# Norm, statistics and moves of rows 3 to 5 reordered at the boundary of a two-stage fp32 layer, and the last element of its first stage

## Chip, cores and metric

The kernel runs on one core of one Trainium2 chip. The metric is the device time of one launch in microseconds (us), the median of the runs shown. It is written in Bass: every engine has its own instruction list in a fixed order, and engines meet only at semaphores, so the order in the source is the order on each engine.

## What is computed

Sixteen batch rows of 128 x 1024 fp32 go through two layers:

```
x = x + tanh(g_xattn) * xattn(layernorm(x), ctx, ctx, Wq, Wk, Wv, Wo, bo, g)
x = x + tanh(g_ffn)   * ffn(layernorm(x), A, B, Wr)

xattn: q = softmax(Wq q) over 64 channels of a head, k = softmax(Wk k) over 1024 positions
       context = k v^T;  out = Wo (context q) + bo
       out / max(sqrt(sum_c out^2), 1e-12) * g * sqrt(128)
ffn:   scores = x Wr^T; the top 16 of 64 experts, softmax over them = gates
       out = sum_k gates_k * B_k (A_k x), rank 16 each; times 2
```

## The kernel before

**Precision.** Every fp32 matmul is done as three passes over operands split into a high part (`_hi`) and a remainder (`_lo`): `three_pass`, lines 61 to 63. ScalarE or a casting DMA makes the high part, VectorE or GpSimd subtracts to get the low part. A matmul group therefore waits for a `lo` step.

**Stage one** (`body` on each engine, b = 0 to 16) does the attention of row b (its head) and the end of row b-1 (its tail). The attention output u of a row goes to DRAM (`u_scratch`). `body(15)` is the last with a head, `body(16)` has only the tail of row 15 and, between its pieces, the first work of stage two: on TensorE context(15), `tr_y(0)`, `tr_q`, `fold(15)` (ends with m_mm), then `up(0, 0)`, the first matmuls of row 0 of stage two. `up(0, 0)` waits for y_lo, which VectorE's `lo_y(0)` sets.

**Stage two** (`ffn_body`, b = 1 to 15) runs on TensorE as `up(b, 0)`, `up(b, 1)`, `up(b, 2)` and `down(b - 1)`: 72 and 48 matmuls. Around it, for row b:

- The norm of u of row e = b+2: ScalarE squares u (`square_u`: line 748 into usq, line 749 scales u), VectorE sums it (`part_u`, line 1190), TensorE adds over partitions with one small matmul pair (`sum_u`, line 1520), VectorE takes the reciprocal root in 11 steps (`norm_step`, lines 969 to 977 and 67, each 128x32) and spreads it (`spread`, line 992), GpSimd multiplies u by it and adds x (`residual`, lines 522 and 525) and so makes the row x2.
- The statistics of x2 on VectorE (`stats2`, lines 1060, 1062 and `std2`), the normalising on ScalarE (`normalise`, line 761), a turn of 32x32 blocks on VectorE (`turn_y`, 1150), 16 block moves on ScalarE (`move_y`, 776), high part (793) and low part (`lo_moved_y`, 1154). `up(b, 0)` waits for this low part.
- The gates on VectorE (`route`, 11 steps, lines 1087 to 1119), the gated product (`gated`, 1134), and the same turn, moves, high (802) and low part (`lo_moved_h`, 1172) for h. `down(b)` waits for this low part.

**The first rows are special.** Rows 0 and 1 get their norm early, with reciprocal roots by GpSimd (`early_newton`). For them VectorE spreads the root (`spread`, into rb_first[0] and rb_first[1]), GpSimd multiplies (`spread_first(e)`, line 506, ends with u_done) and adds x (`add_first(e)`, line 516, ends with x2_done). The tile x_second lies at the same address as rb_first[1]. SyncE fills it with x of row 1 only after u_done has reached 2:

```
sp.wait_ge(u_done, 1)
load(u_first[:, :], u_dram, 1, second_loaded)
sp.wait_ge(u_done, 2)
load(x_second[:, :], x, 1, xr_loaded[1])
```

`add_first(1)` reads x_second and waits for xr_loaded[1]. Behind it on GpSimd come `halve(15, 3)` (line 444), whose result VectorE's `sum_q(15, 3)` (line 1007) waits for, and `normalise(15, 2)` and `(15, 3)`. `lo_y(0)` on VectorE (line 1145) stands behind `sum_q(15, 3)` and itself waits for x2_done of row 1.

At the start of stage two GpSimd makes the low parts of six strips of B (`lo_b`, line 481, 128x1024 each, one behind the other) and VectorE those of two (line 1051).

Of the kernel before, what the change touches and what calls it, by code (L numbers as in the profile page):

```python
# [6 lines left out]
def flamingo_layer(nc, x, ctx, ctxT, g_xattn, g_ffn, WqT, WkT, Wv, WoT, bo, g, AT, BT, u_dram, turn_dram, out):  # L7
# [26 lines left out]
    NEWTON = 3  # L34
# [53 lines left out]
    with outer:  # L88
# [308 lines left out]
        def _(pool):  # L397
# [129 lines left out]
            def body(b, head, tail, ahead, split=False):  # L527
# [11 lines left out]
                if head and not ahead:  # L539
                    spread_first(0)  # L540
                if tail:
                    pool.wait_ge(m_hi, b)
                    nc.gpsimd.tensor_tensor(mts[1][:, :, :], mt[:, :, :], mts[0][:, :, :].bitcast(f32),
                                            ALU.subtract).then_inc(m_lo, 1)
                if split:
# [3 lines left out]
                if head and not ahead:  # L549
                    add_first(0)  # L550
# [3 lines left out]
                if head and not ahead:  # L554
                    for t in range(3):
                        hi_a(t)
                if ahead:
# [5 lines left out]
                if head and not ahead:  # L563
                    spread_first(1)
# [11 lines left out]
                if head and not ahead:  # L576
                    add_first(1)
# [42 lines left out]
        def _(act):  # L620
# [121 lines left out]
            def square_u(e, half, uses):  # L742
# [4 lines left out]
                act.wait_ge(n_part, e)  # L747
                nc.scalar.activation(usq[:, :], u_in[half][:, :], ACT.Square).then_inc(u_sq, 1)
                nc.scalar.activation(u_in[half][:, :], u_in[half][:, :], ACT.Copy,
                                     scale=gcol[:, 0:1]).then_inc(u_scaled, 1)  # L750
# [154 lines left out]
            def ffn_body(i, j):  # L905
# [12 lines left out]
                if not isinstance(i, int) or b <= NB - 4:  # L918
# [12 lines left out]
        def _(dve):  # L931
# [260 lines left out]

            def norm_u(e):

                before = NRT * (e - EARLY)
                for k in range(NRT):
                    norm_step(k, e - EARLY + 2, psN.unsqueeze(1), 1, before)
                dve.wait_ge(x2_done, e)
                spread(0, rb, n_step, before + NRT)
# [13 lines left out]
            def body(b, head, tail, ahead, early=False):  # L1213
# [17 lines left out]
                if tail and head:  # L1231
# [36 lines left out]
                if last:  # L1268
                    dve.wait_ge(xn_lo, 2 * NB)
                    spread(1, rb_first[1], n_newton, 4 * NEWTON)  # L1270
# [39 lines left out]
                if last:  # L1310
                    std2(0, range(4, NCH + 1))
                if head:
# [419 lines left out]
```

## Time and profile before

| what | value |
|---|---|
| median of 3 runs | 930.25 us (928.26 to 930.46) |
| the profiled execution, own time | 932.08 us |
| its span in the trace | 930.4 us |
| PE (TensorE matmul) busy | 901.6 us, 97% |
| DVE (VectorE) busy | 739.7 us, 80% |
| ACT (ScalarE) busy | 684.3 us, 74% |
| POOL (GpSimd) busy | 520.0 us, 56% |
| mean granted TensorE clock | 0.993 |

PEld is TensorE's weight load, SP is SyncE with its DMA queue. In the 40 slices of the page, TensorE is at 9 tenths or more in nearly all, with one slice of 6 tenths at about 605 to 628 us where the granted clock is also below full. Times below are microseconds from the start of the span. A row of the trace that ends in "[3.67 <-DVE yT_lo L1154]" tells how long the engine stood idle before it and what released it. Stage one ends at about 533 us, body(16) runs from there to 557 us, and `ffn_body(1)` starts at 557.07 us.

### The profile page before, as it was taken

The numbers are of one execution on the slowest core, as the hardware profiler recorded it, in microseconds if no ns is written. First come the engines' busy times: TensorE is split into PE (matmuls) and PEld (weight loads), VectorE is DVE, ScalarE is ACT, GpSimd is POOL, SyncE is SP. The second block draws the span as 40 slices with busy tenths as digits, with TensorE's granted clock in tenths as the row PEclk, the third lists the DMA queues.
The fourth block names the chain that finished last, engine by engine and source line by source line (L and its number), as shares of the span: only waits on it lengthen the run. The fifth ranks groups of instructions, "written<-read, shape, count | busy, mean of one in ns | idle before, by whom it ended". The sixth has DMA issues, their size and how long they took to land.

```text
span 930.4 us, 15943 instructions
## 1 busy us (share of the span) xinstructions
PE 901.6 (97%) x4732; PEld 764.7 (82%) x4732; DVE 739.7 (80%) x1523; ACT 684.3 (74%) x1400; POOL 520.0 (56%) x342
## 2 busy tenths in 40 slices
PE   7899999999999999999999999969999999999998
PEld 5687888878787787888887798869999999999896
DVE  6888889988888898898887778777777777777642
ACT  4787787777778777876876758687888888888731
POOL 3686778789778878977789856221222222222200
PEclk9999999999999999999999999979999999999999
DMA  4323423452453444233322784111111211111001
GB/s 158 114 91 125 173 103 124 161 173 100 161 182 106 146 137 159 90 137 135 119 89 87 230 329 154 46 68 68 69 69 68 69 68 68 68 68 68 23 24 46
DMA packets 35319, 104.04 MB, mean 112 GB/s; under 512 B 4432, under 2 KB 11600, under 8 KB 35280
## 3 DMA queue, kind: packets, MB, share of 16 engines
q1 hardware_dynamic: 29520, 82.59, 25.2%
q0 software_dynamic: 5472, 20.45, 6.9%
q10 hardware_dynamic: 288, 0.52, 0.2%
q8 instruction: 19, 0.31, 0.1%
q14 instruction: 20, 0.16, 0.1%
HBM read 79.43 MB, written 24.12 MB: 111 GB/s over the span
## 4 chain that ended last, share of the span: by engine, by line
PE 63%; DVE 9%; POOL 8%; issue 8%; ACT 7%; DMA 2%; SPq 0%; POOLq 0%; ACTq 0%; DVEq 0%
PE ps L61 19%; PE ps L63 18%; PE ps L62 18%; PE ps L1455 3%; PE ps L1464 3%; POOL qe L451 2%; ACT h_raw L776 2%; ACT qe L683 2%; POOL ctx_lo L410 2%; PE ps L1445 1%; DMA turn_scratch<-ek 1%; POOL qhalf L444 1%; POOL aT_lo L464 1%; ACT qT_hi L691 1%; DVE qmax L1002 1%
## 5 line engine op out<-in xcount | busy, mean ns | idle before, releaser
L522 POOL TENSOR_TENSOR rb<-u_in,rb 128x1024 f32<-128x1024 f32 x14 | 33.7, 2409 | 224.7 <-DVE rb L992 224.7
L451 POOL TENSOR_TENSOR qe<-qe,qrec 128x1024 f32<-128x1024 f32 x64 | 121.3, 1906 | 16.3 <-DVE qrec L1010 16.3
L61 PE MATMUL ps<-aT_hi,yT_hi 128*128 128x448 f32 (+2 forms) x360 | 121.1, 337 | 3.7 <-DVE yT_lo L1154 3.7
L62 PE MATMUL ps<-aT_hi,yT_lo 128*128 128x448 f32 (+2 forms) x360 | 119.7, 332 | 0.0
L63 PE MATMUL ps<-aT_lo,yT_hi 128*128 128x448 f32 (+2 forms) x360 | 119.4, 332 | 0.0
L776 ACT ACTIVATE h_raw<-hg 32x256 f32<-32x256 f32 x248 | 103.0, 415 | 16.8 <-DVE hg L1159 14.0
L444 POOL TENSOR_TENSOR qhalf<-qe 128x512 f32<-128x512 f32 x64 | 82.3, 1286 | 57.8 <-ACT qe L683 55.9
L1016 DVE TENSOR_TENSOR qT_lo<-ps,qT_hi 128x512 fp32r<-128x512 f32 x128 | 81.5, 679 | 34.7 <-ACT qT_hi L691 34.2
L776 ACT ACTIVATE y_raw<-u_in 32x256 f32<-32x256 f32 x224 | 92.9, 415 | 4.8 <-DVE u_in L1150 2.4
L61 PE MATMUL ps<-bT_hi,hT_hi 128*128 128x512 f32 x240 | 93.7, 390 | 0.3 <-DVE hT_lo L1172 0.3
L62 PE MATMUL ps<-bT_hi,hT_lo 128*128 128x512 f32 x240 | 93.5, 390 | 0.0
L63 PE MATMUL ps<-bT_lo,hT_hi 128*128 128x512 f32 x240 | 93.4, 389 | 0.0
L676 ACT ACTIVATE qe<-ps 128x1024 f32<-128x1024 f32 x48 | 49.6, 1033 | 52.9 <-PE ps L1445 52.7
L996 DVE TENSOR_REDUCE kmax<-ps 128x1 f32<-128x1024 f32 x64 | 78.0, 1219 | 10.5 <-PE ps L63 8.3
L691 ACT ACTIVATE qT_hi<-ps 128x512 fp32r<-128x512 f32 x128 | 69.5, 598 | 14.0 <-PE ps L1464 14.0
L61 PEld LDWEIGHTS ps<-aT_hi,yT_hi 128*128 128x128 f32 x360 | 69.2, 192 | 6.7 <-DVE yT_lo L1154 4.1
L668 ACT ACTIVATE ek<-ps,kmax 128x1024 f32<-128x1024 f32 x64 | 72.1, 1127 | 3.0 <-DVE kmax L996 3.0
L698 ACT ACTIVATE ekT_hi<-ps 128x512 fp32r<-128x512 f32 x100 | 54.8, 605 | 22.1 <-PE ps L1455 21.5
L62 PEld LDWEIGHTS ps<-aT_hi,yT_lo 128*128 128x128 f32 x360 | 69.3, 192 | 2.2
L63 PEld LDWEIGHTS ps<-aT_lo,yT_hi 128*128 128x128 f32 x360 | 69.1, 192 | 1.9
L1464 PE MATMUL ps<-ident,qe 128*128 128x128 f32 x512 | 67.2, 274 | 1.5 <-DVE ekT_lo L1027 1.5
L1464 PEld LDWEIGHTS ps<-ident,qe 128*128 128x128 f32 x512 | 59.2, 140 | 10.7 <-POOL qe L451 1.4
(179 smaller groups left out, 2558.8 us busy)
## 6 DMA issues: line engine op xcount, KB each, us to landing
x_in<-in_x SPq DMA_DIRECT2D x16, 512.0 KB, 3.3
ctx_in<-in_ctx SPq DMA_DIRECT2D x16, 512.0 KB, 5.4
ctxT_in<-in_ctxT SPq DMA_DIRECT2D x16, 512.0 KB, 3.3
ctxT_hi<-in_ctxT POOLq DMA_DIRECT2D x16, 512.0 KB, 4.1
u_scratch<-osb SPq DMA_DIRECT2D x16, 512.0 KB, 3.0
x<-in_x SPq DMA_DIRECT2D x15, 512.0 KB, 3.8
out<-res SPq DMA_DIRECT2D x15, 512.0 KB, 2.9
turn_scratch<-ek SPq DMA_DIRECT2D x14, 512.0 KB, 4.3
```

Of the source, the lines that this page charges most:

```text
L61: nc.tensor.matmul(psum, whi, mhi, start=start, stop=False)
L62: nc.tensor.matmul(psum, wlo, mhi, start=False, stop=False)
L63: return nc.tensor.matmul(psum, whi, mlo, start=False, stop=stop)
L444: nc.gpsimd.tensor_tensor(qhalf[:, p % 2, :].rearrange("p (h d) -> p h d", d=DH // 2), v[:, :, 0:DH // 2], v[:, :, DH // 2:DH], ALU.add).t ...
L451: nc.gpsimd.tensor_tensor(v, v, w, ALU.mult).then_inc(q_norm, 1)
L668: nc.scalar.activation(to, of, ACT.Exp, bias=kmax[:, j:j + 1], accum_out=ksum[:, j:j + 1]).then_inc(k_exp, 1)
L691: nc.scalar.activation(qT[0][:, :, n * P:n * P + P], psT[:, h, :].rearrange("p (j n) -> p j n", n=P), ACT.Copy).then_inc(q_hi, 1)
L698: nc.scalar.activation(ekT[0][:, 4 * h:4 * h + 4, j * P:j * P + P], psT[:, h, :].rearrange("p (n d) -> p n d", d=P), ACT.Copy).then_inc(k_ ...
L776: last = nc.scalar.activation(dst[32 * q:32 * q + 32, 256 * a:256 * a + 256], src[32 * a:32 * a + 32, 256 * q:256 * q + 256], ACT.Copy)
L996: nc.vector.tensor_reduce(kmax[:, j:j + 1], psK, axis=AX.XY, op=ALU.max, negate=True).then_inc(k_max, 1)
L1016: nc.vector.tensor_tensor(qT[1][:, :, v], psT[:, h, :].rearrange("p (j n) -> p j n", n=P), qT[0][:, :, v].bitcast(f32), ALU.subtract).then ...
L1464: last = nc.tensor.transpose(psT[:, h, j * P:j * P + P], qe[:, p, w:w + P], ident[:, :])
```

## The change

Nothing is computed differently; only orders change. SyncE's list stays as it is.

- GpSimd, body(15): `spread_first(0)` goes behind the mt_lo subtraction, `add_first(0)` behind the first three casting DMAs of A, and `spread_first(1)` from ahead of `normalise(15, 1)` to the end of the body, directly ahead of `add_first(1)`.
- VectorE, body(15): `sum_q(14, 3)` goes behind `max_q(15, 0)` and `max_k(15, 1)`; the spread of row 1's root goes from ahead of `max_k(15, 3)` to behind the last statistics steps of row 0.
- TensorE, body(15): the last of the four matmul groups of `output(14, 0)` goes behind `tr_q(14, 3)`.
- VectorE, stage two: `part_u(3)` goes ahead of `lo_b`; the norm steps of row 3 go from the end of `ffn_body(1)` to its start, seven of them ahead of `lo_moved_h(0)`, and its spread ahead of `gated(1)`; `lo_moved_y(2)` goes ahead of `turn_h(1)`; `result(0)`, `part_u(4)` and `lo_moved_h(1)` go from the end of `ffn_body(1)` into `ffn_body(2)`, `norm_u(4)` into the middle of its route steps; `part_u(5)` goes ahead of `lo_moved_h(2)`.
- ScalarE: the square of u(4) goes ahead of `move_h(1)`, its scaling behind `normalise(3)`; `exp_scores(2)` goes ahead of `normalise(3)`.
- TensorE, stage two: `sum_u(3)` goes from behind `up(1, 1)` to behind `up(1, 0)`, `sum_u(5)` from behind `up(3, 0)` to behind `up(3, 1)`.

```diff
 # GpSimd, body
-                if head and not ahead:
-                    spread_first(0)
                 if tail:
                     pool.wait_ge(m_hi, b)
                     nc.gpsimd.tensor_tensor(mts[1][:, :, :], mt[:, :, :], mts[0][:, :, :].bitcast(f32),
                                             ALU.subtract).then_inc(m_lo, 1)
+                if head and not ahead:
+                    spread_first(0)
...
-                if head and not ahead:
-                    add_first(0)
                 if head:
                     normalise(b, 0)
                     hi_c(b)
                 if head and not ahead:
                     for t in range(3):
                         hi_a(t)
+                    add_first(0)
...
-                if head and not ahead:
-                    spread_first(1)
                 if head:
                     normalise(b, 1)
...
                 if head and not ahead:
+                    spread_first(1)
                     add_first(1)
 # ScalarE, ffn_body
+                if isinstance(i, int) and b == 2:
+                    exp_scores(2)
...
-                exp_scores(b)
+                if isinstance(i, int) and b == 2:
+                    square_u(4, 0, 2, (1,))
+                else:
+                    exp_scores(b)
...
+                if isinstance(i, int) and b == 1:
+                    square_u(4, 0, 2, (0,))
                 move_h(b)
 # VectorE
-                if tail and head:
+                if tail and ahead:
                     sum_q(b - 1, 3)
...
+                if last:
+                    sum_q(b - 1, 3)
                 if last:
                     dve.wait_ge(ctx_lo, 2 * NB)
                     spread(0, rb_first[0], n_newton, 4 * NEWTON)
...
                 if last:
                     std2(0, range(4, NCH + 1))
+                    dve.wait_ge(xn_lo, 2 * NB)
+                    spread(1, rb_first[1], n_newton, 4 * NEWTON)
...
             turn_h(0)
+            part_u(EARLY)
             lo_b(0)
             lo_b(1)
-            part_u(EARLY)
             std2(2, range(NCH + 1))
             for n in range(3):
                 route_step(1, n)
+            norm_steps(3, range(7))
...
                 if first:
                     lo_moved_h(0)
                     turn_y(2, 0)
+                    norm_steps(3, range(7, NRT))
                     for n in range(3, TOP):
                         route_step(1, n)
+                    spread_u(3)
                 elif second:
+                    result(0, 0, 0, 0)
+                    part_u(4)
+                    for n in range(3):
+                        route_step(2, n)
+                    lo_moved_h(1)
                     turn_y(3, 1)
-                    route(2)
                     norm_u(4)
+                    for n in range(3, TOP):
+                        route_step(2, n)
...
+                if first:
+                    lo_moved_y(2)
                 turn_h(b)
-                if ahead:
+                if ahead and not first:
                     lo_moved_y(b + 1)
-                if first:
-                    norm_u(3)
-                    result(0, 0, 0, 0)
-                    part_u(4)
-                    lo_moved_h(1)
 # TensorE
-                    output(b - 1, 0, range(CH // 2, CH))
+                    output(b - 1, 0, range(CH // 2, CH if ahead else CH - 1))
...
+                if tail and not ahead:
+                    output(b - 1, 0, range(CH - 1, CH))
...
-                late = isinstance(i, int) and b <= 2
+                late = isinstance(i, int) and 2 <= b <= 3
```

The order on the engines at the two places of which the prediction speaks. First GpSimd in body(15), before the change (L506 is spread_first, L516 add_first, L451 normalise, L444 halve, L472 a casting DMA of A):

```order
L506 TENSOR_TENSOR u_first<-u_first,rb_first_101 128x1024 [waits n_spread,u_scaled]
L451 TENSOR_TENSOR qe<-qe,qrec 128x1024 [waits q_rec]
L472 DMA aT_hi<-in_AT 128x1088 [waits k_T,q_mm,k_mm] x5
L444 TENSOR_TENSOR qhalf<-qe 128x512 [waits q_sum,q_exp]
L516 TENSOR_TENSOR x_1_106<-x_second,u_first 128x1024 [waits u_done,xr_loaded1]
```

and in the changed kernel:

```order
L451 TENSOR_TENSOR qe<-qe,qrec 128x1024 [waits q_rec]
L472 DMA aT_hi<-in_AT 128x1088 [waits k_T,q_mm,k_mm] x5
L444 TENSOR_TENSOR qhalf<-qe 128x512 [waits q_sum,q_exp]
L506 TENSOR_TENSOR u_first<-u_first,rb_first_101 128x1024 [waits n_spread,u_scaled]
L516 TENSOR_TENSOR x_1_106<-x_second,u_first 128x1024 [waits u_done,xr_loaded1]
```

Between the multiply of row 1 and its add there were a product, five DMA issues and a half sum; now there is nothing.

Second, VectorE at the start of stage two, before the change, from the third route step of row 1 (the first is L1087) to the low part of h(0) and the turn of y(2):

```order
L1093 TENSOR_SCALAR neg_top<-top 128x1 [waits top_step]
L1172 TENSOR_TENSOR hT_lo<-h_raw,hT_hi 128x1024 [waits h_hi]
L1150 STREAM_TRANSPOSE u_in_103<-u_in_103 128x1024 [waits y_done]
L1096 MATCH_REPLACE rest<-top,sc 128x64 [waits top_step]
L1099 MAX top<-rest 128x8 [waits top_step]
```

and in the changed kernel, where L976 to L984 and L67 are the norm steps of row 3 (L969 to L977 and L67 before) and L1179 is the low part of h(0):

```order
L1100 TENSOR_SCALAR neg_top<-top 128x1 [waits top_step]
L976 TENSOR_SCALAR ns<-ps 128x32 [waits n_sum]
L67 TENSOR_SCALAR nr<-ns 128x32 [waits n_step]
L980 TENSOR_TENSOR nt<-nr,ns 128x32 [waits n_step]
L982 SCALAR_TENSOR_TENSOR nt<-nt,nr 128x32 [waits n_step]
L984 SCALAR_TENSOR_TENSOR nr<-nt,nr 128x32 [waits n_step]
L980 TENSOR_TENSOR nt<-nr,ns 128x32 [waits n_step]
L982 SCALAR_TENSOR_TENSOR nt<-nt,nr 128x32 [waits n_step]
L1179 TENSOR_TENSOR hT_lo<-h_raw,hT_hi 128x1024 [waits h_hi]
L1157 STREAM_TRANSPOSE u_in_103<-u_in_103 128x1024 [waits y_done]
L984 SCALAR_TENSOR_TENSOR nr<-nt,nr 128x32 [waits n_step]
```

Seven norm steps now stand ahead of the low part for which `down(0)` waits.

## Rows read from the trace of the kernel before

**Rows 1.** TensorE's waits from 560 to 800 us: total, times, longest

```profile
PE ps L1520 <- DVE part L1190: 4.6, 1, 4.6
PE ps L61 <- DVE yT_lo L1154: 3.7, 1, 3.7
PE ps L61 <- DVE hT_lo L1172: 0.3, 1, 0.3
```

**Rows 2.** Stretches of stage two: length, PE busy, PEclk, DMA share, GB/s

```profile
569.67:580.70 11.03, 11.03 (x48) 1.00 0.14 48
...
607.66:611.00 3.34, 3.34 (x9) 0.51 0.00 1
...
618.94:624.60 5.66, 5.66 (x18) 0.50 0.01 1
...
639.80:662.90 23.10, 23.10 (x124) 1.00 0.20 69
```

**Rows 3.** Timeline of GpSimd in body(15) and the start of body(16)

```profile
511.95 1.91 POOL L451 TENSOR_TENSOR qe<-qe,qrec 128x1024 f32<-128x1024 f32 x1 [0.77 <-DVE qrec L1010]
...
519.94 2.38 POOL L506 TENSOR_TENSOR u_first<-u_first,rb_first 128x1024 f32<-128x1024 f32 x1
...
525.54 2.72 POOL L472 DMA_DIRECT2D aT_hi<-in_AT  x5 [0.46 <-issue]
...
529.50 2.45 POOL L516 TENSOR_TENSOR x<-x_second,u_first 128x1024 f32<-128x1024 f32 x1
533.30 1.29 POOL L444 TENSOR_TENSOR qhalf<-qe 128x512 f32<-128x512 f32 x1 [1.36 <-ACT qe L683]
```

**Rows 4.** DMA issues, 495 to 560 us: KB each, median us to landing

```profile
u_scratch<-osb SPq DMA_DIRECT2D x2, 512.0 KB, 6.6
...
x_second<-in_x SPq DMA_DIRECT2D x1, 512.0 KB, 3.1
```

**Rows 5.** Timeline of VectorE around body(15) to body(16)

```profile
513.84 1.24 DVE L992 STREAM_TRANSPOSE rb_first<-nr 128x1024 f32<-128x1024 f32 x1
...
528.45 0.21 DVE L1073 TENSOR_SCALAR nb<-mv,y 128x1 f32<-128x1 f32 x1
...
534.64 0.68 DVE L1007 TENSOR_REDUCE qsum<-qhalf 128x16 f32<-128x512 f32 x1
...
535.52 1.22 DVE L1145 TENSOR_TENSOR yT_lo<-ps,yT_hi 128x512 fp32r<-128x512 f32 x2
```

**Rows 6.** Timeline of TensorE: end of fold(15) and start of up(0, 0)

```profile
536.46 0.28 PE L63 MATMUL ps<-wvo_lo,kc_hi 128*128 128x256 f32 x1
536.80 0.47 PE L61 MATMUL ps<-aT_hi,yT_hi 128*128 128x448 f32 x1
```

**Rows 7.** Timeline of VectorE in ffn_body(1)

```profile
565.19 0.15 DVE L1093 TENSOR_SCALAR neg_top<-top 128x1 f32<-128x1 f32 x1
567.16 2.45 DVE L1172 TENSOR_TENSOR hT_lo<-h_raw,hT_hi 128x1024 fp32r<-128x1024 f32 x1 [1.82 <-ACT hT_hi L802]
...
572.04 2.30 DVE L1110 TENSOR_TENSOR gsel<-gsel,ex 128x64 f32<-128x64 f32 x1
...
574.83 1.84 DVE L1119 TENSOR_SCALAR gate<-gsel,grec 128x64 f32<-128x64 f32 x1
```

**Rows 8.** GpSimd's low parts of B: all six, then one of them alone

```profile
561.40 15.22 POOL L481 TENSOR_TENSOR bT_lo<-b_raw,bT_hi 128x1024 fp32r<-128x1024 f32 x6 [2.93 <-DMA bT_hi<-in_BT]
```

```profile
571.84 2.42 POOL L481 TENSOR_TENSOR bT_lo<-b_raw,bT_hi 128x1024 fp32r<-128x1024 f32 x1
```

**Rows 9.** Steps by tile (gsel, nt): duration ns min/median/max, first and last start

```profile
L1110 DVE TENSOR_TENSOR gsel<-gsel,ex x16: 224/225/2301, 546.9 to 900.6; 128x64 f32<-128x64 f32 x16
```

```profile
L973 DVE TENSOR_TENSOR nt<-nr,ns x39: 191/192/195, 580.8 to 857.6; 128x32 f32<-128x32 f32 x39
```

**Rows 10.** ScalarE between the two waits: normalise(3), the moves of y(3)

```profile
594.58 1.24 ACT L761 ACTIVATE u_in<-x,nb,y 128x1024 f32<-128x1024 f32 x1 [5.31 <-DVE nb L1073]
...
598.06 6.81 ACT L776 ACTIVATE y_raw<-u_in 32x256 f32<-32x256 f32 x16
```

More of the change, by code:

```diff
@@ L740, in scale_first, with square_u @@
                 nc.scalar.activation(u_first[:, :], u_first[:, :], ACT.Copy, scale=gcol[:, 0:1]).then_inc(u_scaled, 1)
-            def square_u(e, half, uses):
+            def square_u(e, half, uses, steps=(0, 1)):
                 act.wait_ge(u_loaded[half], 16 * uses)
@@ L746, in square_u @@
                     act.wait_ge(q_T, 8 * NB)
[L747 to L750, printed above, removed]
+                if 0 in steps:
+                    act.wait_ge(n_part, e)
+                    nc.scalar.activation(usq[:, :], u_in[half][:, :], ACT.Square).then_inc(u_sq, 1)
+                if 1 in steps:
+                    nc.scalar.activation(u_in[half][:, :], u_in[half][:, :], ACT.Copy,
+                                         scale=gcol[:, 0:1]).then_inc(u_scaled, 1)
             def normalise(b, slot):
@@ L916, in ffn_body @@
                     hi_moved_y(b + 1)
+                if isinstance(i, int) and b == 1:
+                    square_u(4, 0, 2, (0,))
                 move_h(b)
-                if not isinstance(i, int) or b <= NB - 4:
+                if not isinstance(i, int) or 2 <= b <= NB - 4:
                     square_u(b + 3, j % 2, 2 * i + (j + 4) // 2)
@@ L1191, in part_u, with norm_steps, spread_u @@
                                         op=ALU.add, apply_transpose=True).then_inc(n_part, 1)
-            def norm_u(e):
[L1195 to L1199, printed above, removed]
+            def norm_steps(e, steps):
+                for k in steps:
+                    norm_step(k, e - EARLY + 2, psN.unsqueeze(1), 1, NRT * (e - EARLY))
+            def spread_u(e):
+                dve.wait_ge(x2_done, e)
+                spread(0, rb, n_step, NRT * (e - EARLY + 1))
+            def norm_u(e):
+                norm_steps(e, range(NRT))
+                spread_u(e)
             stats(0)
@@ L1267, in body @@
                     lo_q(b - 1, 2)
-                if last:
-                    dve.wait_ge(xn_lo, 2 * NB)
-                    spread(1, rb_first[1], n_newton, 4 * NEWTON)
                 if head:
@@ L1346, in ffn_body @@
                 second = isinstance(i, int) and b == 2
+                third = isinstance(i, int) and b == 3
                 if first:
@@ L1349, in ffn_body @@
                     turn_y(2, 0)
+                    norm_steps(3, range(7, NRT))
                     for n in range(3, TOP):
                         route_step(1, n)
+                    spread_u(3)
                 elif second:
+                    result(0, 0, 0, 0)
[3 more added lines that the diff above has]
+                    lo_moved_h(1)
                     turn_y(3, 1)
-                    route(2)
                     norm_u(4)
+                    for n in range(3, TOP):
+                        route_step(2, n)
                 else:
                     result(b - 2, (j + 1) % 2, (j + 3) % SLOTS, 2 * i + (j - 1) // 2)
+                    if third:
+                        part_u(5)
                     lo_moved_h(b - 1)
-                    if norms:
+                    if norms and not third:
                         part_u(b + 2)
```

## The prediction

> **What bounds the kernel now.** I read the page first: TensorE is busy for 901.6 of 930.4 us, so only its idle stretches and its slow stretches can be won. The list of TensorE's waits shows where they lie in stage two: after 560 us there are three, 4.6, 3.7 and 0.3 us [rows 1], and none after 620 us. The table of stretches adds what each wait costs afterwards. After the 3.7 us wait the clock stands at 0.51 of full (the 1.2 GHz level) for 3.34 us, after the 4.6 us wait at 0.50 for 5.66 us; an undisturbed body takes 23.10 us, and a `down` 11.03 us [rows 2]. From the start of `down(0)` at 569.67 to the start of `up(4, 0)` at 639.80 pass 70.13 us where 2 x 23.10 + 11.03 = 57.2 would do: 12.9 us is what these two waits cost with their slow stretches. That is the most that the reordering of stage two can give. From there to the end TensorE has no wait of this kind, so whatever TensorE gains or loses before 640 us moves the end by the same amount.
>
> **Why the two waits exist.** Row 3's norm steps run last in `ffn_body(1)`, so its x2 is late, `normalise(3)` starts after ScalarE sat idle 5.31 us, and the moves of y(3) start at 598.06 and take 6.81 us [rows 10]; `up(3, 0)` gets its low part only at 607.6. The second wait is `sum_u(5)` behind `up(3, 0)`, whose part comes late. The change starts row 3's norm early, splits the square of u(4) off, and puts `sum_u(5)` one piece later (4.2 us later). With the durations of the trace both waits then vanish: I come back to the slack below.
>
> **Part 1, body(15), where GpSimd and VectorE are reordered.** On VectorE `sum_q(14, 3)` no longer holds up `max_q(15, 0)`, and the spread of row 1 (1.24 us, [rows 5]) leaves the middle of the body. Adding up VectorE's and TensorE's steps in their new order, both come to context(15) about 1.9 us earlier. I value this at nothing, because of what comes next.
>
> GpSimd before took 20.0 us from the start of `normalise(15, 0)` at 511.95 to the end of `add_first(1)` at 531.95 [rows 3]. Up to `halve(15, 2)` it now does the same without `spread_first(1)` (2.38) and `add_first(1)` (2.45), with `add_first(0)` (2.42) added, and without two short waits (0.31 for a DMA, 0.85 for qrec) that now fall into other work: 16.4 us. It starts at 511.2, as VectorE gives qrec 0.75 us earlier, and is through at 527.6. VectorE's spread of row 1 now follows the last statistics of row 0, which ended at 528.66 [rows 5]; 1.9 us earlier plus 1.24 gives 528.0. `spread_first(1)` then takes 2.38 us [rows 3] and ends at 530.4, where before it ended at 522.3. Only then may SyncE load x_second, which lies on rb_first[1]. Before, this load was hidden by 7 us of other GpSimd work. Now `add_first(1)` is the very next instruction on GpSimd, and GpSimd stands still for the whole transfer. Queued behind it are `halve(15, 3)`, both last normalisations and the mt_lo step; SyncE's store of u(14) is behind the load too, which nobody needs soon.
>
> The transfer took 3.1 us when little else ran, and a store among traffic 6.6 us [rows 4]; five transfers of A have just been issued, and the median of such loads of x on the page is 3.8 us. I take 3.8: landing at 534.2. Then 2.45 (`add_first(1)`) and 1.29 (`halve(15, 3)`) [rows 3] give 538.0, against 534.6 before. From `sum_q(15, 3)` to the end of `lo_y(0)` and the start of `up(0, 0)` it is 534.64 to 536.80, 2.16 us [rows 5, 6]. So `up(0, 0)` starts at 540.2 in place of 536.80: **3.4 us later**. TensorE, which before came straight from fold(15) [rows 6], now stands idle for over 5 us there, and I charge it the slow stretch that followed both of its long waits: half of 3.34 or of 5.66 us at half clock, 1.7 or 2.8, mean **2.2 us** [rows 2]. Part 1 costs 5.6 us; between its ends (landing after 3.1 us and 1.7 us of slow clock; landing after 6.6 us and 2.8) 4.4 to 9.0.
>
> **Part 2, the norm steps ahead of `lo_moved_h(0)`.** Alone, a norm step takes 0.19 us, 0.225 from start to start [rows 9], and seven of them (1.6 us) would fit into the 1.82 us in which VectorE waited for the high part of h(0) [rows 7]. But in that stretch GpSimd runs its six low parts of B, 561.40 to 576.6, each 2.42 us, without a gap [rows 8]. The trace shows what a VectorE step with two SBUF inputs does then: the product of line 1110, 128x64, takes 225 ns in the median of 16 and 2301 ns in the one case beside GpSimd, from 572.04 until the GpSimd instruction of 571.84 to 574.2 had ended [rows 7 to 9]. In the same way `lo_moved_h(0)` took 2.45 us, about 1.2 more than in the other rows, and the scaling of line 1119, with one SBUF input, 1.84 in place of 0.25 [rows 7]. Each of them waited for the end of one GpSimd instruction, then ran at once. Tiny 128x1 steps and steps that read PSUM did not wait.
>
> Of the seven norm steps the first reads PSUM and is free; the other six are of the waiting kinds: one like line 1119, five with two SBUF inputs of 128x32. They depend on each other, so between two of them GpSimd gets its next instruction in, and each costs one whole GpSimd instruction. They start at 565.5. The second step waits until 567.2, the next four until 569.7, 572.3, 574.8 and 577.4, when GpSimd is through; the seventh is free. `lo_moved_h(0)` then runs from 577.8 to 579.0, where it ended at 569.6 before. `down(0)` starts **9.4 us later**, and the idle stretch before it brings another slow stretch, **2.2 us** (1.7 to 2.8). If only the two plain products among the six wait, it is the bound from below: to 567.2 and 569.7, then `lo_moved_h(0)` until 573.3, so 3.7 us and 1.6 us of slow clock.
>
> The Trainium skill, "SBUF — State Buffer", section "Who interferes with whom", names the mechanism: VectorE and GpSimd share one pair of SBUF ports under an exclusive lock, and a VectorE instruction with two SBUF inputs, or in a two-port mode, takes part in it while GpSimd reads SBUF. It speaks against this change. The 2301 ns row agrees with it; without it one would read 0.19 us per step and forecast a gain, the first rival below.
>
> **Part 3, what the rest of stage two gives.** With `down(0)` at 579.1 and a slow stretch, it ends at 592. VectorE: turn of y(2) 580.2, four norm steps, eight route steps, spread at 584.6, gated 586.0; ScalarE moves y(2) until 587.1, high part 588.3; low part by 590.8 behind GpSimd's residual(3), 1.2 us before `up(2, 0)` wants it. Then x2(3) 589.6, statistics 596.2, result(0) and part_u(4) 598.7, `lo_moved_h(1)` 601.3 (wanted at 604.2), turn of y(3) 602.9, moves until 609.7, low part 612.4 (wanted by `up(3, 0)` at 615.1), part_u(5) 620.3 (wanted at 624.3). So **both old waits and their slow stretches go: minus 12.9 us**, and no other takes their place.
>
> **The sum.** 3.4 + 2.2 + 9.4 + 2.2 - 12.9 = +4.3 us. The profiled execution took 932.08 us, 1.8 us above the median of the runs, and the sum made against it gives 936.4; against the median of 930.25 us it is 934.5 us. By the bounds of the parts this case reaches from +2.5 to +8.5, 932.7 to 939.
>
> **Rivals.**
> - *The norm steps run free beside GpSimd* (chance 0.23). Then `lo_moved_h(0)` stays at 569.6, `up(2, 0)` waits some 0.9 us for a low part that now comes at 581.5, and both old waits are gone: 5.6 + 0.9 - 12.9 = -6.4 us, 923.9 us. For it: 128x32 steps are the smallest of their kind, and the trace has no such step beside GpSimd. Against it: the 128x64 product. It decides at about 4 us: if the six steps lose less than that together, the change gains. This is the other side of my forecast.
> - *Only the two plain products wait* (0.10): 5.6 + 3.7 + 1.6 - 12.9 = -2.0 us, 928.3 us.
> - *The load of x_second is not waited for long*, because VectorE and GpSimd are ahead by more than I found (0.06): with Part 2 as forecast 11.6 - 12.9 - 0.6 = -1.9, 928.4 us; with both gone -12.6, 917.6 us. Against it: the code lets nothing stand between multiply, load and add.
> - *Another wait is added*, since turn_h(1) now stands behind `lo_moved_y(2)` and the slack of y(2) is 1.2 us (0.08): 2 to 5 us more than forecast, up to 941 us.
>
> **How the numbers follow.** The likeliest case has 0.53. The 0.3% of 930.25 that a measurement can tell is 2.8 us, so faster is below 927.5 and slower above 933.0. From the cases: slower is nearly all of the likeliest and half of the last, 0.53; faster the first rival and parts of the second and third, 0.28; within 0.3% 0.19. The range takes in the first rival and the upper bound: 923.0 to 939.5.
>
> **What the changed profile would show.** Part 1: GpSimd's add of row 1 (line 516) with 3 us or more of idle before it, released by the DMA x_second, and a TensorE wait of 4 to 6 us before the first matmul of `up(0, 0)` with the clock near 0.5 after it. Part 2: norm steps of 2 us or more between 565 and 578 us plus the shift of part 1, and a TensorE wait of about 9 us for hT_lo. Part 3: no TensorE wait for yT_lo or for part. I am wrong if the norm steps there read 0.19 us, or if line 516 has no DMA wait.

## The result and the profile after

| | before | changed |
|---|---|---|
| median of 4 runs each | 930.36 us (928.26 to 930.64) | 942.77 us (941.76 to 943.79) |
| the profiled execution, own time | 932.08 us | 942.16 us |
| its span | 930.4 us | 940.4 us |
| mean granted TensorE clock | 0.993 | 0.987 |
| PE busy | 901.6 us | 901.9 us |

The ratio is 1.0138 [1.0119, 1.0158]: the change makes the kernel slower by 12.4 us. Between the two profiled executions it is 10.1 us (spans: 10.0), since the profiled execution of before lay above its median and that of the changed kernel below. The forecast was 934.5 us, slower; the direction came, the time lies above the upper end of 939.5.

TensorE's work is the same to 0.3 us, so again only its waits and slow stretches count. The three longest of its waits in the changed kernel from 480 to 940 us (total, times, longest); the other two, in stage one, are 0.4 and 0.3 us:

```profile
PE ps L61 <- DVE hT_lo L1179: 8.5, 1, 8.5
PE ps L61 <- DVE yT_lo L1152: 7.0, 1, 7.0
PE ps L1544 <- DVE part L1197: 4.3, 1, 4.3
```

The first two are those of Part 2 and Part 1. Before's wait for the low part of y is gone as forecast, but `part` is back (line 1544 is `sum_u`, 1520 before, line 1197 `part_u`): 4.3 us where it was 4.6 [rows 1]. Three rows of TensorE's timeline say where (start, length, idle before it and its releaser):

```profile
540.58 0.74 PE L61 MATMUL ps<-aT_hi,yT_hi 128*128 128x448 f32 x1 [7.01 <-DVE yT_lo L1152]
...
583.34 0.79 PE L61 MATMUL ps<-bT_hi,hT_hi 128*128 128x512 f32 x1 [8.46 <-DVE hT_lo L1179]
...
652.44 0.64 PE L1544 MATMUL ps<-part,sel 128*128 128x32 f32 x2 [4.25 <-DVE part L1197]
```

These are `up(0, 0)`, `down(0)` and `sum_u(6)` behind `up(4, 0)`. Before, the wait was at `sum_u(5)`, one row earlier. The table of stretches (length, PE busy, PEclk, DMA share, GB/s) gives the slow stretches behind them:

```profile
540.58:547.40 6.82, 6.82 (x24) 0.70 1.01 406
583.34:597.05 13.71, 13.71 (x49) 0.79 0.11 38
643.15:652.44 9.29, 5.04 (x26) 0.90 0.31 112
652.44:658.50 6.06, 6.06 (x23) 0.60 0.00 1
658.50:672.95 14.45, 14.45 (x78) 1.00 0.11 38
672.95:696.01 23.06, 23.06 (x124) 1.00 0.20 69
```

The first is `up(0, 0)`, which took 5.06 us before; the second `down(0)`, 11.03 us undisturbed [rows 2]. The third to the fifth are together the body from `up(4, 0)` to `up(5, 0)`: 29.80 us, where an undisturbed one takes 23.06 (the last). Starts on TensorE, before and after, then give the whole account:

| start of | before | after | later by | of it in this stretch |
|---|---|---|---|---|
| `up(0, 0)` | 536.80 | 540.58 | 3.78 | 3.8, the load of x_second |
| the first piece behind it | 541.86 | 547.41 | 5.55 | 1.8, slow clock |
| `down(0)` | 569.67 | 583.34 | 13.67 | 8.1, the norm steps |
| `up(4, 0)` | 639.80 | 643.15 | 3.35 | -10.3, both old waits, less 2.6 of new slow clock |
| `up(5, 0)` | 662.90 | 672.95 | 10.05 | 6.7, the wait at `sum_u(6)` and its slow clock |
| end of the span | 930.4 | 940.4 | 10.0 | nothing |

Up to `up(4, 0)` the forecast of +4.3 us was off by one microsecond. The rest of the 10.0 us came in the one body behind it.

**GpSimd in body(15).** Its timeline in the changed kernel:

```profile
525.07 1.36 POOL L444 TENSOR_TENSOR qhalf<-qe 128x512 f32<-128x512 f32 x1
526.80 2.40 POOL L506 TENSOR_TENSOR u_first<-u_first,rb_first 128x1024 f32<-128x1024 f32 x1 [0.38 <-DVE rb_first L999]
534.83 2.34 POOL L516 TENSOR_TENSOR x<-x_second,u_first 128x1024 f32<-128x1024 f32 x1 [5.62 <-DMA x_second<-in_x]
537.12 1.25 POOL L444 TENSOR_TENSOR qhalf<-qe 128x512 f32<-128x512 f32 x1
538.33 3.77 POOL L451 TENSOR_TENSOR qe<-qe,qrec 128x1024 f32<-128x1024 f32 x2
```

Multiply, 5.62 us of nothing, add: before, the same load landed under 7 us of other GpSimd work [rows 3]. TensorE stood idle for 7.01 us at `up(0, 0)`; without GpSimd's 5.62 it would have been about 1.4 (an estimate, if nothing else had then held up `halve(15, 3)`).

**VectorE ahead of `down(0)`** (its timeline; L976, L67 and L980 to L984 are the norm steps), and GpSimd's low parts of B beside it:

```profile
565.61 4.52 DVE L1058 TENSOR_TENSOR bT_lo<-b_raw,bT_hi 128x1024 fp32r<-128x1024 f32 x2
...
572.98 0.18 DVE L976 TENSOR_SCALAR ns<-ps 128x32 f32<-128x32 f32 x1
573.19 1.60 DVE L67 TENSOR_SCALAR nr<-ns 128x32 int32<-128x32 int32 x1
574.83 2.27 DVE L980 TENSOR_TENSOR nt<-nr,ns 128x32 f32<-128x32 f32 x1
577.13 2.26 DVE L982 SCALAR_TENSOR_TENSOR nt<-nt,nr 128x32 f32<-128x32 f32 x1
579.43 2.26 DVE L984 SCALAR_TENSOR_TENSOR nr<-nt,nr 128x32 f32<-128x32 f32 x1
581.73 0.19 DVE L980 TENSOR_TENSOR nt<-nr,ns 128x32 f32<-128x32 f32 x1
581.95 0.19 DVE L982 SCALAR_TENSOR_TENSOR nt<-nt,nr 128x32 f32<-128x32 f32 x1
582.06 1.22 DVE L1179 TENSOR_TENSOR hT_lo<-h_raw,hT_hi 128x1024 fp32r<-128x1024 f32 x1
```

```profile
566.30 15.34 POOL L481 TENSOR_TENSOR bT_lo<-b_raw,bT_hi 128x1024 fp32r<-128x1024 f32 x6 [2.42 <-DMA bT_hi<-in_BT]
```

The step that reads PSUM is free; the next four last 8.4 us together and end one GpSimd instruction apart. At 581.6 GpSimd is done, and from there the same steps take 0.19 us each.

### The profile page after: what moved, and what is told of

The parts are those of the page before. It is cut to its first block, busy times and chain, and to the rows that moved or that the text cites. A ratio compares the mean times of both kernels' runs of the same rounds, so it can differ in the third digit from the quotient of the medians.

```text
span 940.4 us, 15943 instructions
## 1 busy us (share of the span) xinstructions
PE 901.9 (96%) x4732; PEld 764.8 (81%) x4732; DVE 747.7 (80%) x1523; ACT 683.6 (73%) x1400; POOL 519.1 (55%) x342
## 4 chain that ended last, share of the span: by engine, by line
PE 62%; DVE 10%; POOL 9%; issue 8%; ACT 7%; DMA 2%; SPq 0%; POOLq 0%; ACTq 0%; DVEq 0%
PE ps L61 18%; PE ps L63 18%; PE ps L62 18%; PE ps L1479 3%; PE ps L1488 3%; POOL qe L451 2%; ACT h_raw L776 2%; PE ps L1469 2%; ACT qe L681 1%; DMA turn_scratch<-ek 1%; POOL qhalf L444 1%; POOL ctx_lo L410 1%; POOL aT_lo L464 1%; ACT qT_hi L689 1%; POOL xn_lo L430 1%
## 5 line engine op out<-in xcount | busy, mean ns | idle before, releaser
L451 POOL TENSOR_TENSOR qe<-qe,qrec 128x1024 f32<-128x1024 f32 x64 | 121.4, 1907 | 16.2 <-DVE qrec L1017 16.0
L444 POOL TENSOR_TENSOR qhalf<-qe 128x512 f32<-128x512 f32 x64 | 82.2, 1285 | 55.0 <-ACT qe L681 53.1
```

The costliest lines, as they stand in the source:

```text
L444: nc.gpsimd.tensor_tensor(qhalf[:, p % 2, :].rearrange("p (h d) -> p h d", d=DH // 2), v[:, :, 0:DH // 2], v[:, :, DH // 2:DH], ALU.add).t ...
L451: nc.gpsimd.tensor_tensor(v, v, w, ALU.mult).then_inc(q_norm, 1)
```

## The experiments

Two theories were there at the start. **Theory A**: three costs, each with its own place: the load of x_second, the norm steps held up by GpSimd's instructions, and a wait for `part` that is a matter of where `sum_u(6)` stands. **Theory B** is the same for the first two, but the third is a debt: ScalarE and VectorE lag behind TensorE, and the lag comes due wherever TensorE next needs something early, so that moving one `sum_u` only moves the wait. The medians of before in the three series were 930.54, 931.27 and 931.59 us; each ratio is taken against its own.

### x1: body(15) as before, the rest of the change kept

All moves in body(15) are undone: of GpSimd's three the one that counts is shown, then VectorE's spread of row 1; `spread_first(0)`, `add_first(0)`, `sum_q(14, 3)` and `output(14, 0)` go back in the same way.

```diff
+                if head and not ahead:
+                    spread_first(1)
                 if head:
...
-                    spread_first(1)
                     add_first(1)
...
+                if last:
+                    dve.wait_ge(xn_lo, 2 * NB)
+                    spread(1, rb_first[1], n_newton, 4 * NEWTON)
                 if head:
...
                     std2(0, range(4, NCH + 1))
-                    dve.wait_ge(xn_lo, 2 * NB)
-                    spread(1, rb_first[1], n_newton, 4 * NEWTON)
```

> The changed kernel with all of the body(15) reordering undone (GpSimd, VectorE, TensorE), stage two as changed. Theory: the load of x_second is hidden again, TensorE does not wait before up(0, 0), and up(0, 0) ends 5.5 us earlier than in the changed kernel, so 942.8 - 5.5 = 937.3 us; the waits for hT_lo (8.5 us) and for part (4.3 us) stay. Rival: what TensorE gains there it waits for later, since VectorE and ScalarE set the pace of the first rows: then 941 us or more.

Measured: 935.58 us, 1.0063 [1.0045, 1.0082]. `up(0, 0)` starts at 535.97 without a wait; 8.5 us for hT_lo and 4.5 us for `part` stay. The changed kernel loses 12.4 us against its own series of before and x1 5.0, so putting body(15) back gives 7.4 us, against the 5.55 of the account above. That is 1.7 us below the expected 937.3, and the rival is out. Most of the 1.8 us between 7.4 and 5.55 is in how the executions lie: 0.8 us is the start of `up(0, 0)` itself, 535.97 here for 536.80 in before's profile, though the order up to there is the same (the kernels with that order started it anywhere from 535.59 to 536.80 us); 0.6 us is that the changed kernel's profiled execution lay that far below its median; 0.2 us is the two medians of before, 930.36 and 930.54.

### x2: only `spread_first(1)` and the spread of row 1 put back

Of the changed kernel's moves in body(15) only the two of the diff of x1 are undone; the others stay.

> The changed kernel with only spread_first(1) on GpSimd and the spread of row 1's root on VectorE put back to their old places. Theory: the load of x_second is hidden and the other steps of the body(15) reordering keep the lead of about 2 us that TensorE had at context(15): 942.8 - 5.5 - 2 = 935.3 us. Rival: the lead is lost at GpSimd, whose last work of row 15 comes no earlier: 937.3 us, as with everything undone.

Measured: 935.58 us, 1.0062 [1.0044, 1.0080], the time of x1. So the whole loss of Part 1 lies in these two moves, which put the load between `spread_first(1)` and `add_first(1)` and nothing else. The number is the expected one, but not by the reason given for it: x2 was to lie 2 us below x1 and does not. The other moves in body(15) bring `up(0, 0)` forward, to 534.63, 1.3 us ahead of x1. In the two profiled executions 0.8 us of this is left to the end (spans of 933.1 and 933.9 us), and x2's lay 0.7 us below its median; the medians show nothing of it. A first sign for Theory B is inside this pair. The slow stretch behind the 8.5 us wait was shorter in x2, so that `sum_u(4)` ran 2.3 us ahead of x1 (597.14 and 599.47); `sum_u(6)` ran only 1.3 us ahead (644.74 and 646.06), as far as its `part` was. `part` is waited for 4.8 us in place of 4.5, and a wait of 0.3 us for yT_lo appears: what TensorE wins against its suppliers it stands idle for.

### x3: all eleven norm steps of row 3 behind `lo_moved_h(0)` and the turn of y(2)

```diff
-            norm_steps(3, range(7))
...
                     turn_y(2, 0)
-                    norm_steps(3, range(7, NRT))
+                    norm_steps(3, range(NRT))
```

> The changed kernel with the seven norm steps of row 3 behind the low part of h(0) and the turn of y(2) instead of ahead. Theory (port lock): the low part of h(0) no longer stands behind four blocked steps, the 8.5 us wait shrinks to 1 to 2 us; two of the steps are still blocked by GpSimd, now ahead of the gates, so up(2, 0) waits 2 to 4 us and pays a slow stretch. Together 4 to 6 us less than the changed kernel: 937 to 939 us. Rival (the steps wait for their small matmul or for each other, not for GpSimd): they would be as slow in the new place, all six of them, and the time would stay at 942 us.

Measured: 938.98 us, 1.0096 [1.0079, 1.0113], inside what was expected. The wait for hT_lo falls from 8.5 to 1.0 us, but `up(2, 0)` now waits 4.4 us for yT_lo (line 1161). VectorE's timeline shows the steps still meeting the end of GpSimd's strips, now ahead of the rest of row 1's route, and the low part of y(2) only at 590.41:

```profile
578.32 0.14 DVE L976 TENSOR_SCALAR ns<-ps 128x32 f32<-128x32 f32 x1
578.49 1.03 DVE L67 TENSOR_SCALAR nr<-ns 128x32 int32<-128x32 int32 x1
579.56 2.32 DVE L980 TENSOR_TENSOR nt<-nr,ns 128x32 f32<-128x32 f32 x1
581.92 2.32 DVE L982 SCALAR_TENSOR_TENSOR nt<-nt,nr 128x32 f32<-128x32 f32 x1
584.27 0.19 DVE L984 SCALAR_TENSOR_TENSOR nr<-nt,nr 128x32 f32<-128x32 f32 x1
...
590.41 2.40 DVE L1161 TENSOR_TENSOR yT_lo<-y_raw,yT_hi 128x1024 fp32r<-128x1024 f32 x1
```

Moving the steps moves the loss; it has to be taken away from them.

### x4: `sum_u(6)` one piece later too

```diff
-                late = isinstance(i, int) and 2 <= b <= 3
+                late = isinstance(i, int) and 2 <= b <= 4
```

> The changed kernel with sum_u(6) on TensorE behind up(4, 1) instead of up(4, 0). Theory A: the 4.3 us wait for part with its slow stretch of 2.8 us is a transient of rows 3 to 6 and goes: 942.8 - 7 = 935.8 us. Theory B: VectorE and ScalarE lag TensorE by some 4 us from row 3 on, and without the wait to catch up the lag shows at the next row, sum_u(7): the wait moves and the time stays within 1 us of 942.8.

Measured: 943.13 us, 1.0139 [1.0121, 1.0156], the changed kernel's time. `sum_u(6)` no longer waits; one row later `sum_u(7)` does:

```profile
676.19 0.63 PE L1544 MATMUL ps<-part,sel 128*128 128x32 f32 x2 [3.89 <-DVE part L1197]
```

Theory A falls here, Theory B stands. The same run gives the reason. Three rows of ScalarE and one of VectorE, around the moves of h(3) and h(4):

```profile
640.74 6.82 ACT L776 ACTIVATE h_raw<-hg 32x256 f32<-32x256 f32 x16 [0.50 <-DVE hg L1166]
...
650.74 1.23 DVE L1179 TENSOR_TENSOR hT_lo<-h_raw,hT_hi 128x1024 fp32r<-128x1024 f32 x1 [1.27 <-ACT hT_hi L802]
...
654.95 0.35 ACT L807 ACTIVATE ex<-sc,neg_top 128x64 f32<-128x64 f32 x1 [3.18 <-DVE neg_top L1100]
...
663.68 6.83 ACT L776 ACTIVATE h_raw<-hg 32x256 f32<-32x256 f32 x16 [0.49 <-DVE hg L1166]
```

ScalarE moves h, squares and scales u and makes the high part of h, 9.9 us together; then VectorE, without an idle stretch until 663.65, makes its low part, `part_u`, turns y, and runs the route, the norm steps, the spread, `gated` and the turn of h, 12.9 us together; then ScalarE can move the next h. In this row, in which TensorE does not wait, that loop comes round in 22.94 us, and TensorE's body in 23.06. ScalarE's other work, exp and the moves of y, fits beside it: ScalarE waits 3.18 us ahead of exp and 0.50 us for hg. At a gain of a tenth of a microsecond per row a lag of 4 us is not worked off in the rows left. It is paid once, when TensorE stands still, and after that every row is in step: behind its wait, `part` ends 0.6 to 1.1 us ahead of `sum_u` in every row, in before as in the changed kernel.

### x5: GpSimd starts its strips of B only after the seven norm steps

```diff
+            pool.wait_ge(n_step, 7)
             for k in range(KC):
```

> The changed kernel, but GpSimd starts its six low parts of B only when the seven norm steps are done; VectorE's list is as in the changed kernel. Port lock theory: the seven steps take 0.19 us each again, the low part of h(0) comes some 8 us earlier, and TensorE's wait for it (8.5 us) is gone or below 1 us; instead TensorE waits in down(0) for the late strips of B, 5 us or so. Rival (the steps are slow for a reason on VectorE or at their semaphore): they stay above 2 us.

Measured: 942.23 us, one execution. Same instructions, same order on VectorE, only GpSimd idle meanwhile:

```profile
571.61 0.18 DVE L67 TENSOR_SCALAR nr<-ns 128x32 int32<-128x32 int32 x1
571.83 0.19 DVE L981 TENSOR_TENSOR nt<-nr,ns 128x32 f32<-128x32 f32 x1
572.05 0.19 DVE L983 SCALAR_TENSOR_TENSOR nt<-nt,nr 128x32 f32<-128x32 f32 x1
572.28 0.19 DVE L985 SCALAR_TENSOR_TENSOR nr<-nt,nr 128x32 f32<-128x32 f32 x1
...
573.29 3.20 DVE L1180 TENSOR_TENSOR hT_lo<-h_raw,hT_hi 128x1024 fp32r<-128x1024 f32 x1 [0.37 <-ACT hT_hi L803]
```

So it is GpSimd's work beside them that makes the steps long, not the semaphores between them. It is no cure: GpSimd idles 8.5 us, `down(0)` waits three times for its strips (2.7 us where 5 was expected), and the low part of h(0) takes 3.20 us beside them. `down(0)` starts 6.8 us earlier than in the changed kernel (576.55 for 583.34), but `sum_u(6)` only 0.4 us (652.02 for 652.44), after a wait of 4.9 us: again TensorE's gain is not its suppliers'.

### x7: two of the norm's three tiles in PSUM, the order of the change kept

```diff
                 s, r, t = (v[:, 0:count, :] for v in (ns, nr, nt))
+                if isinstance(before, int) and before == 0:
+                    s, t = ps[:, 3, 32:64].unsqueeze(1), ps[:, 3, 64:96].unsqueeze(1)
```

> The changed kernel with two of the three small tiles of row 3's norm steps in PSUM, so that no step has two SBUF inputs; the order of all instructions is unchanged. Port lock theory: none of the steps waits for GpSimd, each takes 0.2 to 0.3 us, the low part of h(0) comes 4 to 7 us earlier (it can itself be blocked once), TensorE's wait for it falls from 8.5 to 2 to 4 us: 942.8 - 5 to 7 = 936 to 938 us. Rival (the lock is not about SBUF inputs): steps stay above 2 us, 943 us.

Measured: 936.30 us, 1.0061 [1.0042, 1.0080]. GpSimd is in the middle of its six strips (566.63 to 583.3), and the steps are free:

```profile
573.70 0.19 DVE L67 TENSOR_SCALAR nr<-ps 128x32 int32<-128x32 int32 x1
573.92 0.20 DVE L982 TENSOR_TENSOR ps<-nr,ps 128x32 f32<-128x32 f32 x1
574.15 0.20 DVE L984 SCALAR_TENSOR_TENSOR ps<-ps,nr 128x32 f32<-128x32 f32 x1
574.39 0.19 DVE L986 SCALAR_TENSOR_TENSOR nr<-ps,nr 128x32 f32<-128x32 f32 x1
...
574.95 1.39 DVE L1181 TENSOR_TENSOR hT_lo<-h_raw,hT_hi 128x1024 fp32r<-128x1024 f32 x1
```

hT_lo is waited for 1.0 us in place of 8.5. Against the medians of before in their own series the changed kernel loses 12.4 us and x7 loses 5.0, so Part 2 is worth 7.4 us net; of the 8.1 us and the slow stretch at `down(0)` some returns as two waits of 1.4 and 1.5 us for the low part of y, and the wait for `part` is 4.9 us in place of 4.3. Row 1's route steps now run beside GpSimd's strips (lines 1115 and 1119, the two products of gsel, took 1.72 and 2.32 us for 0.23 each in the changed kernel), which may be why; no run tests it.

### x6 and x8: `part_u` behind three route steps, and `sum_u` late

To shorten the suppliers' loop and give them more room, in x6 (the changed kernel) and x8 (before), `part_u` stands behind the turn of y and three route steps, and `sum_u` behind `up(b, 1)` in every row (in x6 all but b = 1).

```diff
-                    if norms and not third:
-                        part_u(b + 2)
                     if ahead:
                         turn_y(b + 1, j % 2)
-                    route(b)
+                    for n in range(3):
+                        route_step(b, n)
+                    if norms and not third:
+                        part_u(b + 2)
+                    for n in range(3, TOP):
+                        route_step(b, n)
...
-                late = isinstance(i, int) and 2 <= b <= 3
+                late = not (isinstance(i, int) and b == 1)
```

> The changed kernel with, for every row from 4 on, the turn of y and the first three route steps ahead of part_u on VectorE, and sum_u behind up(b, 1) instead of up(b, 0) on TensorE. Lag theory: VectorE and ScalarE run round a loop through exp_scores that takes 22.94 us against TensorE's 23.06, so a lag is never worked off; taking part_u out of it shortens the loop by 1.2 us, sum_u has 4.2 us more room, and the 4.3 us wait for part with its slow stretch goes for good: 942.8 - 7 = 935.8 us. Rival (the wait only moves, as it did with sum_u(6) alone): 942 to 943.5 us.

> The kernel before the change with the same shortening of the loop for rows from 3 on and sum_u behind up(b, 1) throughout. Lag theory: its 4.6 us wait for part with 2.8 us of slow clock goes, the 3.7 us wait for y(3) stays: 930.4 - 7.5 = 922.9 us. Rival: the wait moves to a later row, 930 us.

Measured: x6 937.24 us, 1.0078 [1.0056, 1.0101]; x8 927.49 us, 0.9963 [0.9949, 0.9977]. Right in direction, but less than expected, x8 above all: it gained 3.8 us, half of the expected 7.5. The wait for `part` is 2.0 us in x6 and 2.2 in x8, not gone: `sum_u` comes 4.2 us later, but `part_u` too comes later, by the turn and three short steps, some 2 us. Half of the room is eaten by the other half of the edit. Nor did the loop become 1.2 us shorter: in x6 the low parts of h(3) to h(7) start at 649.69, 672.41, 695.25, 718.19 and 740.92 us, 22.8 us apart in the mean. The expectation had taken the loop to run through exp, but `part_u` still stands in the one that x4 shows, between the low part of h and its next moves. That called for the late `sum_u` alone.

### x9 and x10: `sum_u` late in every row, nothing else

```diff
 # x9, in the changed kernel
-                late = isinstance(i, int) and 2 <= b <= 3
+                late = not (isinstance(i, int) and b == 1)
 # x10, in the kernel before
-                late = isinstance(i, int) and b <= 2
+                late = True
```

> The changed kernel with sum_u behind up(b, 1) for every row from 4 on and nothing else. Lag theory: the lag of about 4 us at row 6 neither grows nor shrinks (the loop takes 22.94 us, TensorE 23.06), and the room of 4.2 us is now there at every row, so no wait for part is left anywhere: 7 us less than the changed kernel, 935 to 936 us. Rival (late sums feed the norm steps late and the lag grows): a wait of 2 us or more at some later row, 938 us or more.

> The kernel before the change with sum_u behind up(b, 1) for every row and nothing else. Lag theory: its wait for part (4.6 us and 2.8 us of slow clock) is at most 0.5 us, the wait for y(3) stays: 7 us less than before, 923 to 924 us. Rival (the wait moves): less than 2 us gained.

Measured: x9 936.09 us, 1.0049 [1.0032, 1.0066]; x10 924.34 us, 0.9927 [0.9911, 0.9944]. Both within 0.4 us of what was expected. In x9 the wait for `part` is 0.7 us, still at `sum_u(6)`, and none follows; in x10 one wait is left in stage two:

```profile
PE ps L61 <- DVE yT_lo L1154: 3.7, 1, 3.7
```

In x9 the loop still comes round in 22.94 us (moves of h at 641.08 and 664.02), and over more rows not even that gain stays: `part` ends at 653.46 in row 6 and at 861.07 in row 15, 23.07 us per row. The lag has not gone; it has stopped costing, since in every row it fits into the 4.2 us, if barely. In row 7 of x9 `part` ends at 676.40:

```profile
675.16 1.24 DVE L1197 TRANSPOSE_TENSOR_REDUCE part<-usq 128x32 f32<-128x1024 f32 x1
...
676.66 0.30 PE L1544 MATMUL ps<-part,sel 128*128 128x32 f32 x2
```

That is 0.26 us ahead of `sum_u(7)`, and in the rows behind it is 0.1 to 0.5 us; at its old place, 4.2 us earlier, `sum_u(7)` would have waited 3.9 us, what it waited in x4. One row with room (`late` for b = 2 and 3 in the change, for b = 4 in x4) only passes the wait to the first row without. And x10 shows that before's own 4.6 us wait was this same debt: one changed line in the kernel before gives 7.2 us, and its `part` ends 0.4 to 1.2 us ahead in rows 5 and up.

### x11: the change with all three costs taken away, and x12: before with what is good in the change

x11 is the changed kernel with the edits of x2, x7 and x9. x12 is the kernel before with `late = True` and with the moves in body(15) that x2 had kept.

> The changed kernel with its three costs taken away: spread_first(1) and its spread back, the norm steps of row 3 in PSUM, sum_u behind up(b, 1) for every row from 4 on. If the three are independent: 942.8 - 7.2 - 6.5 - 7 = 922 us, 8 to 9 us faster than before. Rival: with TensorE earlier, VectorE and ScalarE become the bound of the first rows and part of it comes back as waits for yT_lo: 925 to 928 us.

> The kernel before the change with sum_u behind up(b, 1) for every row and those parts of the body(15) reordering that x2 kept. Theory: 7 us from the late sums and 1 to 2 us from body(15): 921.5 to 923 us. Rival: the lead from body(15) turns into a longer wait for y(3): 923 to 924 us, no more than the late sums alone.

Measured: x11 **922.40 us** (922.13 to 923.10), 0.9904 [0.9888, 0.9921]; x12 923.24 us, 0.9916 [0.9899, 0.9933]. x11 is where its expectation put it: the three costs are independent to about 1 us. Each is the loss of the changed kernel against its before, less that of the mended one against its own: 7.4 us for x2, 7.4 for x7, 7.9 for x9, together 22.7; taking them off +12.4 gives -10.3, and x11 measured -9.2. Its waits in stage two, 535 to 700 us:

```profile
PE ps L61 <- DVE yT_lo L1164: 3.0, 2, 1.6
PE ps L61 <- DVE hT_lo L1182: 1.0, 1, 1.0
PE ps L1548 <- DVE part L1200: 0.7, 1, 0.7
```

None is longer than 1.6 us, and the granted clock of x11's profiled execution is 1.000 in the mean, where the changed kernel has 0.987 and x12, with one wait of 3.7 us, 0.998.

x11 beats both kernels, and x12 by less than the runs can separate (the intervals overlap). So whether the reordering of stage two, rid of its costs, is worth anything beside a kernel before that has one line of stage two changed and the same body(15) is not shown; the medians differ by 0.8 us. x12 itself lies 1.1 us below x10, with overlapping intervals, just above its expectation and in the range of its rival. The rival's mechanism did not come: the wait for y(3) is 3.7 us in both.

## Why the prediction was right and wrong

- **Part 1** (forecast 3.4 us later and 2.2 of slow clock, 5.6): measured 3.78 and 1.77, 5.55. Right, though in two of its steps by luck: `spread_first(1)` ended at 529.2 where 530.4 was forecast, since the lead at context(15) was 3.1 us (524.49 for 527.64) and not 1.9; the load took 5.5 us from issue to landing where I took 3.8, between 3.1 and 6.6 [rows 4]. Of the two ends the upper one was nearer: the DMA engines were busy throughout it (share 1.05 from 529.3 to 534.8), where before's load had met a share of 0.48 (522.3 to 525.5). The earlier start and the longer load nearly cancel. x2 shows that the two moves alone make the loss; that most of it is the load is read from the timeline.
- **The lead of body(15), "valued at nothing"**: by the medians of x1 and x2 it is worth nothing, by their profiled executions 0.8 us, and by x12 against x10 1.1 us; none of these is clear of noise. The reason I gave, the load, is not all of it, since x2 has no such wait and gains no more.
- **Part 2** (forecast `down(0)` 9.4 us later, 2.2 of slow clock): measured 8.1 and 2.6. The mechanism is what x5 and x7 show. The term was 1.3 us too large: four steps were blocked, not five, because VectorE's own two strips ahead of them took 4.52 us and the steps began later against GpSimd's six. I had put this piece at its old length. The rule of the Trainium skill that the prediction weighed ("SBUF — State Buffer", section "Who interferes with whom") decided rightly against the 0.19 us row [rows 9]: a VectorE instruction with two SBUF inputs contends with a GpSimd one that reads SBUF, and the trace agrees (line 980, 2.27 us). The rivals "run free" (0.23) and "only the two plain products wait" (0.10) fell: line 67, with one SBUF input, took 1.60 us, and each scalar_tensor_tensor 2.26.
- **Part 3** is the step that failed: "both old waits and their slow stretches go: minus 12.9 us, and no other takes their place". The first half holds to the tenth. From `down(0)` to `up(4, 0)` the changed kernel took 59.81 us; less 57.23 of undisturbed work this is 2.58, all of it the slow stretch of Part 2, and nothing of the 12.9 is left. The second half is wrong. I followed the steps in order up to the one that used to be late, `part_u(5)` against `sum_u(5)`, and stopped at a body that was undisturbed before. The forecast's own numbers held the sign: they give `sum_u(5)` 4.0 us of slack (part at 620.3, wanted at 624.3), less than the 4.2 us that it had got by moving, so nothing was left for a row that did not move. Measured, the slack was 1.8 us (627.39 and 629.15). `sum_u(6)`, left where it was, needed what `sum_u(5)` had needed, and its `part_u` stands behind the low part of h again (1.2 us), ahead of which `part_u(5)` had been put. Before, TensorE had already paid by waiting 4.6 us and everything behind was in step. With the payment put off, the row after had to make it: 4.25 us, and 2.5 of slow clock. The net gain of Part 3 was 12.9 - 6.7 = 6.2 us.
- **The sum** becomes 5.55 + 8.1 + 2.6 - 12.9 + 6.7 = 10.05, the difference between the spans. The remaining 2.3 us to the 12.4 between the medians is how the two profiled executions lie to their medians, 1.7 above and 0.6 below.
- **The rival "another wait is added"** (0.08) was the true kind of case, at the wrong place (turn_h(1) against y(2), which TensorE did not wait for) and with too low a chance. Its upper end, 941, stands on the sum for the profiled execution (936.4 + 5); on the median it is 934.5 + 5 = 939.5, the end of the range, so the range held nothing for a wait with a slow stretch of its own.

What stays open: why kernels with the same order up to there start `up(0, 0)` up to 1.2 us apart, and why waits of the same length are followed by slow stretches of different length.

## What to carry to other kernels

A wait removed in one row of this pipeline came back in the next, since the supplier's loop is not shorter than the consumer's by enough to catch up. Compare the two periods (here 22.94 and 23.06 us in one row, equal to 0.1 us over nine rows of x9) and follow the slack past the last wait of the old profile, since the first row without the new room inherits the old wait. Give such room to all rows or to none: the one line that did this was worth 7.2 us in the kernel before (x10). Before moving two instructions of one queue together, look for what another queue does between them (here a load into the first one's input tile), and before moving small VectorE steps beside a run of GpSimd instructions, count each that has two SBUF inputs, and each tensor_scalar of 128x32 or more from SBUF, as up to one GpSimd instruction, or put a tile in PSUM. Steps of 128x1 did not wait.

## What the runs showed of the hardware

- One input in PSUM is enough. A 128x32 step with one input in each memory (line 982 in x7) takes 0.20 us beside GpSimd's strips, the same step with two SBUF inputs 2.27 (line 980 of the changed kernel). Before's trace had the like at 128x512: line 1145, from ps and yT_hi, took 1.22 us for two [rows 5] while GpSimd normalised (534.54 to 538.32).
- A VectorE tensor_scalar with one SBUF input waited as well: 128x32 int32 (line 67) 1.60 us, 0.18 with GpSimd idle. Two strips of 128x1024 on VectorE took 4.52 us for 2.31 in x5.
- The load of x_second, 512 KB, landed after 5.5 us here and 3.1 before [rows 4].
- Of the clock: in stage two every wait of 3.7 us or more was followed by a stretch at about half clock; the waits of up to 1.6 us in x11 and of 2.0 us in x6 by none, but the one of 2.2 us in x8 by a clock of 0.50 from 621 to 624 us. Short waits close together are another case: in x5 waits of 0.3, 1.4 and 1.0 us ahead of three matmuls of one `down` were followed by 4.85 us at 0.50.
- The length of the slow stretch is not set by that of the wait alone: behind the same 8.5 us wait it was 2.7 us in x9, 3.1 in x2, 5.7 in the changed kernel and 6.1 in x4.
